# The end of attention written out step by step: the last batch's reciprocals formed on TensorE, two output banks and four x buffers from row group 50

## The reference

```python
x = x + _L0_xattn_ref(_layernorm(x), ctx_1024, ctx_1024, Wq, Wk, Wv, Wo)
x = x + _L0_ffn_ref(_layernorm(x), w_gate, w_up, w_down)
# in _L0_xattn_ref:
score = jnp.einsum('bhqd,bhkd->bhqk', qh, kh) * scale      # qh, kh after rope
attn = jax.nn.softmax(score, axis=-1)
out = jnp.einsum('bhqk,bhkd->bhqd', attn, vh)
return jnp.einsum('bsd,de->bse', out, Wo)
# in _L0_ffn_ref:
x = act_qdq(x)        # scale = max(abs(x)) / 32767 over the whole tensor
```

## Time and profile before

| what | us |
|---|---|
| median of 3 runs | 2397.19 |
| the profiled execution | 2395.11 |
| its span | 2393.3 |
| PE busy in the span | 2244.4 |
| last product with V starts (unit 63) | 793.06 |
| last row group's output done, then the maximum on PE | 843.1, 850.67 |
| gate stage starts | 854.20 |

### The profile page before, as it was taken

How to read it: one execution, slowest core, us unless ns; L and a number is a source line. 1 busy time by engine, 2 the same in 40 slices (tenths; PEclk the granted TensorE clock), 3 DMA queues, 4 the chain that set the end, 5 groups by cost and what they waited for, 6 DMA issues and landing times. The chain is left out here.

```text
span 2393.3 us, 32283 instructions
## 1 busy us (share of the span) xinstructions
PE 2244.4 (94%) x12833; PEld 1007.4 (42%) x12833; DVE 1673.1 (70%) x1703; ACT 1283.1 (54%) x1191; POOL 703.3 (29%) x493
## 2 busy tenths in 40 slices
PE   5898999999998689999999999999999599999999
PEld 3443434444443234444444444444444244444444
DVE  7545788788865466644543289888888777777774
ACT  3335544545443123222332488787777687777772
POOL 3344666656654211000100055444444000000000
PEclk8999999999998889999999999999999799999999
DMA  4434555556666557887876698777777365555552
GB/s 158 120 105 112 171 166 171 169 170 169 177 152 149 137 179 241 273 244 242 266 246 213 196 350 305 285 280 287 289 285 299 148 241 212 211 213 218 216 228 88
DMA packets 287560, 501.35 MB, mean 209 GB/s; under 512 B 187820, under 2 KB 190124, under 8 KB 250540
## 3 DMA queue, kind: packets, MB, share of 16 engines
q1 hardware_dynamic: 286556, 498.09, 63.5%
q10 hardware_dynamic: 848, 1.15, 0.1%
HBM read 248.83 MB, written 186.65 MB: 182 GB/s over the span
## 5 line engine op out<-in xcount | busy, mean ns | idle before, releaser
L1405 PE MATMUL banks<-XB,W 128*128 128x512 f16 x2304 | 499.9, 380 | 2.2 <-ACT XB L1431 2.2
L1405 PE MATMUL banks<-XB,WT 128*128 128x512 f16 x2304 | 499.3, 380 | 2.7 <-ACT OB L1425 2.7
L1853 PE MATMUL banks<-W,OH 128*128 128x512 f16 x2256 | 489.7, 380 | 6.8 <-DVE OH L1947 6.8
L1425 ACT ACTIVATE OB<-banks,uns 128x512 f32<-128x512 f32 x384 | 255.2, 684 | 395.6 <-PE banks L1405 393.1
L1405 PEld LDWEIGHTS banks<-XB,W 128*128 128x128 f16 x2304 | 225.9, 98 | 275.9 <-issue 4.7
L1405 PEld LDWEIGHTS banks<-XB,WT 128*128 128x128 f16 x2304 | 225.7, 98 | 276.1 <-ACT OB L1425 3.2
L1853 PEld LDWEIGHTS banks<-W,OH 128*128 128x128 f16 x2256 | 221.3, 98 | 275.2 <-DVE OH L1947 7.3
L1687 POOL TENSOR_TENSOR PR<-GS,OB 128x2048 f32<-128x2048 f32 x46 | 220.7, 4798 | 262.0 <-ACT OB L1425 242.8
L1514 DVE TENSOR_REDUCE amx<-OB 128x1 f32<-128x2048 f32 x48 | 109.7, 2285 | 239.9 <-ACT OB L1425 239.9
L827 ACT ACTIVATE P<-banks 120x2048 f32<-120x2048 f32 x64 | 119.9, 1873 | 160.0 <-PE banks L594 160.0
L657 PE MATMUL banks<-XC,AH 128*128 128x512 f16 x768 | 184.6, 393 | 18.8 <-DVE RX L1070 18.8
(11 more groups left out here) (243 smaller groups left out, 2899.6 us busy)
## 6 DMA issues: line engine op xcount, KB each, us to landing
g_s<-OB SPq DMA_DIRECT2D x48, 1024.0 KB, 6.5
GL<-g_s SPq DMA_DIRECT2D x48, 1024.0 KB, 8.0
up_s<-OB SPq DMA_DIRECT2D x48, 1024.0 KB, 4.9
XA<-up_s SPq DMA_DIRECT2D x32, 1024.0 KB, 9.3
gq_s<-GQ SPq DMA_DIRECT2D x48, 512.0 KB, 5.1
...
QW<-QE SPq DMA_DIRECT2D x128, 128.0 KB, 2.9
```

Of the source, the lines that this page charges most:

```text
L1405: t = e.matmul(pk[:].rearrange("p (j t) -> p j t", j=4), WT[w][:, ot, wa, kk, :], XB[i % 2][:, xa, :, kk, :], start=(kk == 0 and wa == 0 a ...
L1425: e.activation(OB[n % 3][:, r, :], bank[(k + 4) % 8][:], ACT.Copy, scale=uns[:, 12 * w + ot:12 * w + ot + 1]).then_inc(s_ev, 1)
L1853: t = e.matmul(pk[:].rearrange("p (r n) -> p r n", r=4), OH[i % 2][:, a, ot, j * 128:(j + 1) * 128], WD[:, :, c, wa, o4, :], start=(ot == ...
```

## The change

Steps stop at 66 (`NSTEP` = 67); everything after is written out on each engine.

- From row group 50 (`LATE`) outputs alternate between two banks, and x and x1 use four buffers (`x_of`): two of RX's and the freed rope tiles QE and QW. Step 65 takes two row groups (49 and 50), so every later one comes a unit earlier.
- The gate-weight transposes start in step 57 in place of 60 (`sp_gate_turn`); the last two stand behind batch 14's reciprocal loads.
- Batch 14's reciprocals go into four QR tiles in place of the two RB tiles.
- Batch 15's products with V go to AZ. Its reciprocals no longer pass through DRAM: PE transposes RC into `BS_`, DVE takes the reciprocals, ACT spreads each over 32 columns into P, PE multiplies by the identity (`pe_recip`, a transpose by matmul) into banks 6 and 7, and DVE multiplies AZ by that bank, in four parts of 128 tokens (`dve_last`). ACT and POOL form high and low parts by the same four parts, and row group 60+j waits for part j alone.
- DVE takes the row groups one by one, each with its statistics at once (`row_group`).

```diff
-NSTEP = NU + 13
-LATE = NU - 8
+NSTEP = NU + 3
+LATE = NU - 14
...
 def normal_at(s):

     b, c = divmod(s - 13, 4)
-    if s == NSTEP - 4:
-        return list(range(NU - 4, NU))
-    return [4 * b + 2 * c, 4 * b + 2 * c + 1] if 0 <= b < B - 1 and c < 2 else []
+    return [4 * b + 2 * c, 4 * b + 2 * c + 1] if 0 <= b < B - 2 and c < 2 else []
...
 def output_at(s):

-    u = s - 16
-    if u < LATE:
-        return [u] if u >= 0 else []
-    u = LATE + 2 * (u - LATE)
-    return [u, u + 1] if u < NU else []
+    if s < 16:
+        return []
+    return [s - 16] if s < NU + 1 else [[LATE - 1, LATE], [LATE + 1], [LATE + 2]][s - NU - 1]
...
-            i = u - NU + 4
-            return QR[i][:], s_rb[i], 16 * ((NU - 4) // 2 + 1) if i < 2 else 16
+            i = u - NU + 8
+            return QR[i][:], s_rb[i], 16 * ((NU - 8) // 2 + 1) if i < 2 else 16
+
+        AZ = f32(XD[1][:])
+        RT = RG[:].rearrange("p (j g c) -> p j g c", j=4, g=4)
...
+        def x_of(u):
+
+            if u < LATE:
+                return RX[:, u % 2, :], RX[:, 2 + u % 2, :], u % 2, 16 * (u // 2 + 1)
+            m, i = divmod(u - LATE, 4)
+            xr, x1 = ((QE[0][:], QW[0][:]), (QE[1][:], QW[1][:]), (RX[:, 0, :], RX[:, 2, :]), (RX[:, 1, :], RX[:, 3, :]))[i]
+            return xr, x1, i, 16 * (m + 1 + (LATE // 2 if i < 2 else 0))
...
-            if u >= NU - 4:
+            if u >= NU - 8:
                 e.wait_ge(s_c1, NU - 4)
...
+        def sp_x1_out(e, u):
+
+            _, x1, i, _ = x_of(u)
+            e.wait_ge(s_x1, u + 1)
+            e.dma_start(x1_d[u // 4, :, u % 4, :], x1).then_inc(s_x1d[i], 16)
+
+        def sp_xr_load(e, u):
+            xr, _, i, _ = x_of(u)
+            if u < 2:
+                e.wait_ge(s_wlo, 4)
+            elif u < LATE:
+                e.wait_ge(s_x1, u - 1)
+            elif u < LATE + 2:
+                e.wait_ge(s_rm1, len(ROTS))
+                e.wait_ge(s_qw[0], 32 * ((len(ROTS) + 1) // 2))
+                e.wait_ge(s_qw[1], 32 * (len(ROTS) // 2))
+            else:
+                e.wait_ge(s_x1, u - 3)
+            e.dma_start(xr, x1_rows(u // 4)[:, u % 4, :]).then_inc(s_xr[i], 16)
+
+        def sp_gate_turn(e, t):
+
+            e.wait_ge(s_c1, 48)
+            e.wait_ge(s_ws, 16 * (t + 1))
+            e.dma_start_transpose(WT0[:, t, :, :, :].rearrange("p a k o -> p (a k) o"),
+                                  wt_d[0, t].rearrange("o a i -> o (a i)")).then_inc(s_wt0, 16)

...
-
-                if 60 <= s < 60 + NO:
-                    t = s - 60
-                    e.wait_ge(s_c1, 48)
-                    e.wait_ge(s_ws, 16 * (t + 1))
-                    e.dma_start_transpose(WT0[:, t, :, :, :].rearrange("p a k o -> p (a k) o"),
-                                          wt_d[0, t].rearrange("o a i -> o (a i)")).then_inc(s_wt0, 16)
+                if s >= 57:
+                    sp_gate_turn(e, s - 57)
...
+            dma_sums_out(e, B - 2)
+            sp_x1_out(e, LATE + 1)
+            sp_xr_load(e, LATE + 3)
+            sp_xr_load(e, LATE + 4)
+            dma_sums_in(e, B - 2)
+            sp_x1_out(e, LATE + 2)
+            sp_xr_load(e, LATE + 5)
+            dma_recip_out(e, B - 2)
+            sp_x1_out(e, LATE + 3)
+            sp_xr_load(e, LATE + 6)
+            for u in range(NU - 8, NU - 4):
+                dma_recip(e, u)
+            sp_gate_turn(e, NO - 2)
+            sp_gate_turn(e, NO - 1)
+            for u in range(LATE + 4, NU):
+                sp_x1_out(e, u)
+                if u + 3 < NU:
+                    sp_xr_load(e, u + 3)
...
+            if b == B - 1:
+                e.wait_ge(s_x1, LATE + 1)
...
             if u == LATE:
-                e.wait_ge(s_mte, B)
-            elif u > LATE:
+                e.wait_ge(s_qe, len(ROTS))
+            elif u > LATE + 1:
                 e.wait_ge(s_x1, u - 1)
             elif u:
-                e.wait_ge(s_x1, u)
+                e.wait_ge(s_x1, u if u < LATE else u - 1)
             else:
                 e.wait_ge(s_wlo, 4)
                 e.wait_ge(s_vu, 3)
-            if j == 0:
+            if u == LATE + 2:
+                e.wait_ge(s_mte, B)
+            if u >= NU - 4:
+                e.wait_ge(s_alo, u + 1)
+            elif j == 0:
                 e.wait_ge(s_alo, 4 * b + 4)
...
+        def pe_recip(e, j):
+
+            e.wait_ge(s_re, j + 1)
+            if j == 0:
+                e.wait_ge(s_a, NU)
+            elif j >= 2:
+                e.wait_ge(s_an, NU - 4 + j - 1)
+            for c in range(4):
+                t = e.matmul(bank[6 + j % 2][:, c * 128:(c + 1) * 128], P[:, j, c * 128:(c + 1) * 128], id32[:],
+                             start=True, stop=True)
+            t.then_inc(s_rx, 1)
...
@@ -738,11 +788,38 @@
                     pe_values(e, s - 7)
...
-            e.wait_ge(s_a, NU)
+            for u in range(NU - 4, NU):
+                pe_scores(e, u)
+                pe_output(e, u - 8)
+                pe_values(e, u)
+
+            e.wait_ge(s_qn, 4)
+            e.wait_ge(s_p, NU)
+            for j in range(4):
+                for k in range(4):
+                    t = e.transpose(PB[:, j, k * 128:(k + 1) * 128], XA[0][:, j, k * 128:(k + 1) * 128], id32[:])
+            t.then_inc(s_tx, 1)
+
+            pe_output(e, NU - 8)
+            e.wait_ge(s_rc, B)
+            for j in range(4):
+                t = e.transpose(BS_[:, j * 128:(j + 1) * 128], RC[:, j * 128:(j + 1) * 128], id32[:])
+            t.then_inc(s_rt, 1)
+            pe_output(e, NU - 7)
+            pe_recip(e, 0)
+            pe_recip(e, 1)
+            pe_output(e, NU - 6)
+            pe_recip(e, 2)
+            pe_recip(e, 3)
+            for u in range(NU - 5, NU):
+                pe_output(e, u)
+
+
+            e.wait_ge(s_an, NU)
             e.wait_ge(s_g, 1)
-            e.transpose(PB[0:1, 6, 0:128], gm[:, 14:15], id32[:]).then_inc(s_gt, 1)
-            e.wait_ge(s_gx, 1)
...
                         e.wait_ge(s_rg, 64 * (b - 2))
                     e.activation(RC[:], BS_, ACT.Copy).then_inc(s_rc, 1)
-                    if b - 2 == B - 1:
-                        dma_sums_out(e, B - 1)
-                        dma_sums_in(e, B - 1)
-                        dma_recip_out(e, B - 1)
-                        for u in range(NU - 4, NU):
-                            dma_recip(e, u)
                 if s < NU:
                     n = ROT["q", s]
...
                         if k >= 1:
                             e.wait_ge(s_ws, 16 * k)
                         e.activation(w_hl[:, 0, :], w_ld[k % 2], ACT.Copy).then_inc(s_wh, 1)
+
+            u = NU - 5
+            e.wait_ge(s_sum, u + 1)
+            e.wait_ge(s_rg, 64 * (B - 2))
+            e.activation(RC[:], BS_, ACT.Copy).then_inc(s_rc, 1)
+            e.wait_ge(s_pv, u + 1)
+            e.wait_ge(s_alo, u - 5)
+            e.activation(A[:, u % 6, :], BP_, ACT.Copy).then_inc(s_a, 1)
+            for u in range(NU - 4, NU):
+                e.wait_ge(s_c1, u + 1)
+                e.wait_ge(s_sum, u)
+                e.activation(P[0:SK], PB[0:SK, 0:4, :], ACT.Exp, scale=SM_SCALE).then_inc(s_p, 1)
+                if u < NU - 1:
+                    e.wait_ge(s_pv, u + 1)
+                    e.wait_ge(s_q, NU)
+                    e.activation(AZ[:, u - NU + 4, :], BP_, ACT.Copy).then_inc(s_a, 1)
+            for u in range(NU - 8, NU - 4):
+                e.wait_ge(s_an, u + 1)
+                e.wait_ge(s_o, NU - 12)
+                e.activation(AH[(B - 2) % 2][:, 0, u % 4, :], A[:, u % 6, :], ACT.Copy).then_inc(s_ah, 1)
+            e.wait_ge(s_sum, NU)
+            e.wait_ge(s_rg, 64 * (B - 1))
+            e.activation(RC[:], BS_, ACT.Copy).then_inc(s_rc, 1)
+            e.wait_ge(s_pv, NU)
+            e.activation(AZ[:, 3, :], BP_, ACT.Copy).then_inc(s_a, 1)
+            e.wait_ge(s_rr, 2 * B - 1)
...
                 t = e.bn_aggr(mv2[:, 4 * b + i, :], st2[:, b % 2, i, :])
             t.then_inc(s_mv2, 1)
+
+        def dve_x1(e, u):
+
+            xr, x1, i, n = x_of(u)
+            e.wait_ge(s_o, u + 1)
+            e.wait_ge(s_xr[i], n)
+            if LATE <= u < LATE + 2:
+                e.wait_ge(s_radd, len(ROTS))
+            elif u >= 2:
+                last = u - 2 if u < LATE else u - 4
+                _, _, i, n = x_of(last)
+                e.wait_ge(s_x1d[i], n)
+                e.wait_ge(s_st2, 3 * last + 3)
...
+        def dve_last(e, j):
+
+            e.wait_ge(s_rx, j + 1)
+            e.wait_ge(s_a, NU)
+            part = AZ[:, :, j * 128:(j + 1) * 128]
+            e.scalar_tensor_tensor(part, part, vun[:, 1:2], bank[6 + j % 2].rearrange("p (c t) -> p c t", c=4),
+                                   ALU.mult, ALU.mult).then_inc(s_an, 1)

...
+
+
+            def row_group(u):
+                dve_x1(e, u)
+                dve_x1_stats(e, u)
+
+            row_group(NU - 13)
+            row_group(NU - 12)
+            dve_x1_aggregate(e, B - 4)
```

(51 more changed lines are left out.)

152 lines of the change are left out of this document (70 added, 82 removed).

## The result

| | before | changed | ratio, 95% interval |
|---|---|---|---|
| median of the runs, us | 2397.19 | 2383.57 (2372.27 to 2384.73, 5 runs) | 0.9928 (0.9906 to 0.995) |
| the same kernel run once more, us | 2393.95 | 2380.24 (2373.27 to 2382.67, 5 runs) | 0.9944 (0.9931 to 0.9958) |
| profiled execution, us | 2395.11 | 2372.27 | |
| its span, us | 2393.3 | 2370.1 | |

What follows compares the result with a forecast made beforehand. PE, busy 94% of the span, was taken as the bound, with waits around the end of attention. 2395.1 - 2.1 - 16.6 + 5.5 = 2381.9, plus 2.08 for the median, gives 2384.0 us; range 2376 to 2392.

Steps and rivals of the forecast that it cites:

- Batch 14, -2.1 us: End of attention: batch 14's reciprocals land so that row group 56 starts near 798.8 instead of 800.90 us.
- Row group 56 to the maximum, -16.6 us: From row group 56's start on PE to the maximum of x1: 33.2 us instead of 49.8.
- The new chain hides: Batch 15's reciprocals on PE run behind outputs with 4 to 8 us to spare; 15.67 us of wait go.
- The tail: From the last output to the maximum on PE: x1, three passes and the aggregate, 5.9 us.
- the clock behind the wait: After idle PE, row group 56 and the next output take 3.3 us each instead of 2.76: +1.1 us.
- The transposes, +5.5 us: Steps 57 and 58: the earlier gate transpose delays unit 58's swap and so PE, between 3.0 and 11.5 us.
- The rival that the transposes hide: Steps 57 and 58: the earlier transposes cost nothing, giving 2378.5 us; chance 0.18.
- What costs nothing: Transposes 10 and 11, XA loads, four x buffers, wider zero-one tile and pooled semaphores add no time.
- A late batch 14 with a low clock: Rival: batch 14's loads take 16.8 us and the first two outputs 4.49 each, giving 2389 us; chance 0.13.
- DVE does not set the end: Its rival: from row group 56 DVE's passes pile up and lose some 4 us, giving 2388 us; chance 0.06.
- The jams of swaps: Slower rival: transposes in steps 57 to 60 each stall PE, up to 2405 us; chance 0.05 for 2398 and above.

Runs made afterwards that it cites:

- early14: Changed kernel with batch 14's reciprocal ahead of row group 52 on DVE and its SP loads ahead of two x1 stores: 2378.12 us, ratio 0.9935.
- early14b: early14 plus ACT's high part of row group 56 ahead of unit 63's exponential: 2373.56 us, ratio 0.9916.
- dram15: Changed kernel with batch 15's reciprocals through DRAM again, without the spreading matmuls and the four-part split: 2393.18 us, ratio 0.9996.
- onebank: Changed kernel with all outputs from row group 51 on in one PSUM bank: 2378.74 us, ratio 0.9943.
- turns60: Changed kernel with the gate-weight transposes starting in step 60 again: 2377.26 us, ratio 0.9931.
- before57: Kernel before the change with only its gate-weight transposes moved to start in step 57: 2398.59 us, ratio 1.0022.
- twobuf: Changed kernel with two x and two x1 buffers to the end instead of four from row group 50: 2393.10 us, ratio 1.0004.

## Why the prediction was right

The forecast gain was right and its main step too; one step was right in its sum only, one edit was misjudged, and two effects that I did not forecast are of the size of the smaller terms.

*Batch 14, -2.1 us: right.* Measured from Q, which takes out what happened before it, row group 56 starts after 28.45 us (28.6 in the mean of four profiles); the forecast's 798.8 is 28.8 behind its Q, and the kernel before took 31.76 and 30.61. On the absolute scale 798.55 looks exact, but I had expected the shift of the transposes, 5.5 us, on top. The loads went out 10.7 us behind Q where I had 11.1. I had the landing wrong in its parts: the first took 6.5 us, not 4.9, but the further products followed every 2.6 us, not 3.1, since POOL's order and ACT's high parts set them as much as the loads do. early14 and early14b suggest that the chain has two ends: loads sooner alone gave 3.5 us, hardly more than two medians of one kernel differ by, loads and ACT's high part sooner gave 8.0.

*Row group 56 to the maximum, -16.6 us: right.* Measured -16.15 in the first pair, and 17.2 between the means of all profiles (49.73 and 32.52). The new chain hides, as argued. A part on PE costs 0.89 us where I took 0.85 from a transpose and a score product; the Trainium skill, "FP8 and Floating Point Precision", section TensorE Precision Notes, led to an estimate of 0.9, and the trace agrees. The tail took 5.83 us (5.9 predicted). The size that was off is the clock behind the wait: I gave the first two outputs 3.3 us each, 1.1 above the full clock in all, where the profiles show 2.5 in the first and 1.3 in each of the other three; the first output took 5.28, 4.03, 4.11 and 4.04 in the four profiles (granted clock 0.50 in the first of these, 1.2 GHz throughout, and 0.68 in the second), the output behind it 2.75 to 2.78. dram15 puts this step's worth at 11.6 us in the medians, less than the 15.2 of the profiles; the second bank's part (onebank, 4.2 in the profile) is not seen in the medians.

*The transposes, +5.5 us: near in sum, not in its terms.* turns60 and before57 put their price at 4.3 and 4.5 us. I built it as 2.95 us of SP, passed on to PE one for one, and 2.5 us of a slower landing of the swap. What is added ahead of the swap did reach PE nearly one for one: 2.2 us later at the swap's issue behind P, 1.9 at the scores of step 60, where PE waited 1.70, under the 3 to 8 that I had named. But of the two terms the first was too large and the second absent. The transpose itself held SP for 1.27 us, and the swap was used 4.1 us after its issue (681.69 to 685.80), no later than the 4.4 of before. So the profiles show 1.4 to 1.9 us of a price whose medians are 4.3 and 4.5; that these are near 5.5 is luck as far as my working goes, and where the rest arises stays open. I had taken both terms from one transpose, which stood right behind two broadcast loads, while the trace of the kernel before had holds from 1.23 to 7.81 us among its twelve. The Trainium skill, "DMA: Bandwidth & Descriptors", section Latency and other measured facts, with its 261 GB/s for DMA transposes, gives an estimate of 1 us for moving the 256 KB. SP's hold is not the same thing, and only the short holds (1.27 us at 678.54) are near that figure; the 7.78 at 755.33 and the 11.06 for two at 783.63 are not. The rival that the transposes hide falls by before57, whose interval leaves zero out.

*"What costs nothing": failed for the x buffers.* I wrote that of the four x buffers "the loads stand three row groups ahead" and costed them at nothing. That holds for the change as a whole, and the sum is not touched, but twobuf shows that they carry 11.5 us: without them, in this order of SP's queue, the rest of the change is worth nothing. What I overlooked is the other side of the buffer: its release hangs on a store in SP's queue, and SP is held there by gate transposes.

*The medians.* I added 2.08 us because the profile before lay that much below its median. That was a median of three; over the 56 executions of the kernel before that are on record it is 2394.3, under the profile. The profile after lies 11.3 below its own median. Step by step the first pair of profiles gives -23.2 us where I had -13.2. The 10.0 us between them: 1.7 ahead of P, 3.7 in P to Q (2.7 where 6.4 were predicted, 0.9 of it the row group moved to step 65), 3.8 in gate and up, 0.9 in the rest, less 0.1 in the steps between. Of these only the 3.7 belongs to a step of mine; the other 6.4 are in stages whose code the change does not alter. By the large samples the gain is 12.7 us (2394.3 less 2381.6), close to my 13.2; that the time itself came within 0.4 us is luck. Since most profiled executions lie under the median of their series, the steps of a profile do not add up to the medians, and what makes up this difference stays open.

*Other rivals.* A late batch 14 with a low clock (2389) was there in part: the clock was low, batch 14 was not late. DVE does not set the end: its x1 come every 2.57 us up to 826.55 and the last is done 1.0 us behind PE's last output. The jams of swaps did not come: between P and Q of the changed kernel the stall of step 62, as before, is the only one over 2.1 us.
